# Order of the score matmuls in the middle blocks: all four heads' lower 64 keys first, then the upper 64

## The reference: what is computed

```
xq  = ada_ln(x_q,  t_vec, Wss_q,  bss_q)        # layer norm, then scale and bias from silu(cond)
xkv = ada_ln(x_kv, t_vec, Wss_kv, bss_kv)
q   = (xq @ Wq + bq)    -> (1, 4096, 16, 32)
k,v = (xkv @ Wkv + bkv) -> (1, 3202, 16, 32) each
scores = einsum('bqhd,bkhd->bhqk', q, k) / sqrt(32)
attn   = softmax(scores)
out    = x_q + (einsum('bhqk,bkhd->bqhd', attn, v) @ Wp + bp)
```

## Time and profile before

| what | value |
|---|---|
| median of 3 runs | 2154.9 us (2151.96 to 2155.5) |
| the profiled execution | 2154.18 us |
| its span, first to last instruction | 2152.5 us |
| TensorE busy | 2123.1 us (99%) |
| VectorE busy | 1925.8 us (89%) |
| ScalarE busy | 1801.6 us (84%) |
| score matmuls, line 1119 | 12800, busy 920.8 us |
| value matmuls, line 1131 | 6400, busy 853.3 us |
| exponentials, line 1377 | 1600, 1112 ns each |

### The profile page before, as it was taken

The page is one execution under the profiler, slowest core; times in us unless marked ns, Lnnn a source line. Parts: engine busy times, 40 slices in busy tenths (PEclk is TensorE's granted clock), DMA queues, the critical chain, the costliest instruction groups (busy, mean ns, idle before and its releaser), DMA issues.

```text
span 2152.5 us, 56243 instructions
## 1 busy us (share of the span) xinstructions
PE 2123.1 (99%) x25034; PEld 610.7 (28%) x25034; DVE 1925.8 (89%) x1193; ACT 1801.6 (84%) x1923; POOL 17.3 (1%) x28
## 2 busy tenths in 40 slices
PE   7999999999999999999999999999999999999998
PEld 3544322222222222222222222222222222222222
DVE  2335599999999999999999999999999999999998
ACT  1212599999999999999999999999999999999995
POOL 0001000000000000000000000000000000000000
PEclk9999999999999999999999999999999999999999
DMA  8346624223422324223422333233422332232321
GB/s 288 118 149 225 177 73 104 77 77 89 124 67 82 93 74 103 83 72 104 109 82 71 101 95 92 62 84 91 120 77 75 94 96 81 68 85 79 97 55 51
DMA packets 202212, 212.33 MB, mean 99 GB/s; under 512 B 18791, under 2 KB 136175, under 8 KB 201965
## 3 DMA queue, kind: packets, MB, share of 16 engines
q1 hardware_dynamic: 199420, 208.16, 34.6%
q10 hardware_dynamic: 2544, 0.53, 0.1%
HBM read 170.38 MB, written 38.26 MB: 97 GB/s over the span
## 4 chain that ended last, share of the span: by engine, by line
PE 97%; DVE 1%; DMA 1%; issue 0%; SPq 0%; ACT 0%; POOL 0%; ACTq 0%; DVEq 0%
PE bank L1119 40%; PE bank L1131 37%; PE bank L1189 5%; PE bank L1151 5%; PE bank L1035 4%; PE bank L1046 4%; PE bank L1162 1%; PE bank L1015 1%; PE bank L1247 1%; DVE stats L1473 0%; PE bank L1174 0%; DVE arena L1491 0%; DMA x_normal<-arena 0%; DMA arena<-in_ctx_dram 0%; PE bank L988 0%
## 5 line engine op out<-in xcount | busy, mean ns | idle before, releaser
L1377 ACT ACTIVATE arena<-bank,shift 128x1024 f32<-128x1024 f32 x1600 | 1691.7, 1112 | 140.7 <-PE bank L1119 133.8
L1694 DVE TENSOR_TENSOR arena<-arena 128x2048 f32<-128x2048 f32 x736 | 1641.4, 2283 | 67.4 <-ACT arena L1377 65.6
L1119 PE MATMUL bank<-qs,ks 32*64 32x512 f32 x12800 | 920.8, 613 | 4.6 <-ACT arena L1377 4.0
L1131 PE MATMUL bank<-arena,vg 128*32 128x512 f32 x6400 | 853.3, 605 | 1.2 <-ACT arena L1377 1.2
L1131 PEld LDWEIGHTS bank<-arena,vg 128*32 128x32 f32 x6400 | 126.0, 108 | 652.1 <-ACT arena L1377 650.5
L1119 PEld LDWEIGHTS bank<-qs,ks 32*64 32x64 f32 x12800 | 205.7, 130 | 371.0 <-ACT arena L1377 228.1
L1189 PE MATMUL bank<-wp,arena 128*32 128x168 f32 (+2 forms) x2464 | 153.6, 321 | 0.0
L1151 PE MATMUL bank<-xt,wq 128*32 128x256 f32 (+2 forms) x2016 | 143.0, 355 | 0.0
L1189 PEld LDWEIGHTS bank<-wp,arena 128*32 128x32 f32 x2464 | 80.1, 110 | 184.3 <-issue 165.3
L1334 ACT ACTIVATE arena<-bank,bk_c 128x512 f32<-128x512 f32 (+1 forms) x28 | 18.0, 642 | 130.4 <-PE bank L1035 124.1
L1151 PEld LDWEIGHTS bank<-xt,wq 128*32 128x32 f32 x2016 | 65.5, 110 | 150.8 <-issue 132.9
(11 more groups left out here) (89 smaller groups left out, 394.8 us busy)
## 6 DMA issues: line engine op xcount, KB each, us to landing
ks<-k_full SPq DMA_DIRECT2D x160, 320.0 KB, 3.1
vg<-v_full SPq DMA_DIRECT2D x160, 320.0 KB, 3.8
p_b<-p_tails SPq DMA_DIRECT2D x128, 128.0 KB, 4.2
arena<-in_x_dram SPq DMA_DIRECT2D x15, 1024.0 KB, 9.8
q_full<-qs SPq DMA_DIRECT2D x32, 256.0 KB, 2.0
out_dram<-arena SPq DMA_DIRECT2D x32, 256.0 KB, 2.2
x_normal<-arena SPq DMA_DIRECT2D x7, 1024.0 KB, 7.6
xin<-x_normal SPq DMA_DIRECT2D x28, 256.0 KB, 10.3
```

The source lines that it names most:

```text
L1119: mm = nc.tensor.matmul(bank[out, 2 * (i % RING) + h % 2, :], ks[rows_of(h), keys], qs[rows_of(h), g, :], start=True, stop=True)
L1131: mm = nc.tensor.matmul(bank[rows_of(h), o_bank(u), :], vg[:, t, rows_of(h)], pt[t % PR][:, h, :], start=(t == 0), stop=False, skip_group_ ...
L1377: nc.scalar.activation(pt[t % PR][:, 2 * pair:2 * pair + 2, :], bank[:, first:first + 2, :], ACT.Exp, scale=SCALE, bias=shift[:, g:g + 1]) ...
L1694: nc.vector.tensor_tensor(a[:, :, :], (pt[t - 1] if k <= 2 else a)[:, :, :], pt[t % PR][:, :, :], ALU.add).then_inc(p_added, 1)
```

## The change

In blocks 1 to 6 the 8 score matmuls of a step are written in another order. Before: wait for pair 0's banks, heads 0 and 1 of the lower side, heads 0 and 1 of the upper side, wait for pair 1's banks, heads 2 and 3 of the lower side, heads 2 and 3 of the upper side. Now: wait for pair 0's banks, heads 0 and 1 of the lower side, wait for pair 1's banks, heads 2 and 3 of the lower side, heads 0 and 1 of the upper side, heads 2 and 3 of the upper side. `s_ready` is still raised by each pair's last matmul. Blocks 0 and 7 keep the old order; the number of matmuls, their shapes and tiles, and the waits stay.

```diff
-                        for pair in range(2):
+
+                        def score(pair, side):
                             i = n + pair
-                            if i >= RING:
-                                pe.wait_ge(e_done, i - RING + 1)
-                            for side in range(2):
-                                out = slice(side * P // 2, (side + 1) * P // 2)
-                                keys = slice(t * P + side * P // 2, t * P + (side + 1) * P // 2)
-                                for h in (2 * pair, 2 * pair + 1):
-                                    mm = nc.tensor.matmul(bank[out, 2 * (i % RING) + h % 2, :], ks[rows_of(h), keys],
-                                                          qs[rows_of(h), g, :], start=True, stop=True)
-                            mm.then_inc(s_ready, 1)
+                            out = slice(side * P // 2, (side + 1) * P // 2)
+                            keys = slice(t * P + side * P // 2, t * P + (side + 1) * P // 2)
+                            for h in (2 * pair, 2 * pair + 1):
+                                mm = nc.tensor.matmul(bank[out, 2 * (i % RING) + h % 2, :], ks[rows_of(h), keys],
+                                                      qs[rows_of(h), g, :], start=True, stop=True)
+                            if side == 1:
+                                mm.then_inc(s_ready, 1)
+
+                        def banks_free(pair):
+                            if n + pair >= RING:
+                                pe.wait_ge(e_done, n + pair - RING + 1)
+
+                        if 1 <= u // NG < NB - 1:
+                            for pair in range(2):
+                                banks_free(pair)
+                                score(pair, 0)
+                            for pair in range(2):
+                                score(pair, 1)
+                        else:
+                            for pair in range(2):
+                                banks_free(pair)
+                                for side in range(2):
+                                    score(pair, side)
```

## The result

The changed kernel takes 2165.49 us (median of 6 runs, 2161.0 to 2166.99) against 2154.9 us (6 runs, 2151.96 to 2156.34): ratio 1.005, 95% interval 1.004 to 1.006, so 10.6 us slower. The profiled execution has a span of 2163.0 us, 10.5 more than before. The forecast was 2161.7 us, 6.8 more than before; the terms of its sum come to 7.2.

A forecast was written before the change was run, and what follows sets the result against it. TensorE was taken as the bound, short steps held up by a 2.32 us loop through ScalarE's exponential. 2154.18 + 6.4 + 0.8 = 2161.4 us, stated as 2161.7; own range 2157.5 to 2165, 8-in-10 range 2154 to 2168.

The forecast's parts named there:

- The loop of 2.32 us: Scores' start to pair 0's exponential 1.15 us, exponential 1.12, then 0.05 until the next step's pair 1 may start.
- the lost alternation: At unit changes in blocks 1 to 6, held-up and free steps would stop alternating; each behind a short one waits: 6.4 us.
- The 168-column steps lose their margin: In 192 steps with a 168-column side job, pair 1's banks would come free slightly late: 4 ns each, 0.8 us together.
- 2 x 0.007 = 0.014 us later: Pair 0's last score matmul, now sixth instead of fourth, would come this much later, making the loop 2.335 us.
- Unhindered steps unchanged: In some 530 steps without a hold-up the new order would change nothing; zero taken, a gain at most 14 us.
- Rival B: Four heads on four row groups first make the score passes shorter: 14.3 us gained, 2147 us in all; chance 0.07.
- Rival A: Heads 0 and 1 of the upper side pass the waiting head 2, so no change: 2155 us; chance 0.10.
- Rival C: In 66 held-up steps one head's two sides clash on the same rows: 11 us more, 2173 us; chance 0.07.
- VectorE and ScalarE have slack: Behind held-up steps neither engine's work would come due; they work 57.12 and 54.92 us of a 59.30 us unit.

The follow-up runs named there:

- third-place wait: Changed kernel with the old matmul order back in blocks 1 to 6, the wait for pair 1's banks still ahead of the third matmul: 2158.07 us, ratio 1.0024.
- the fifth and the seventh place: Changed kernel with pair 0's last score matmul fifth or seventh of eight in blocks 1 to 6, not sixth: 2160.01 and 2166.77 us.
- head-by-head order: Kernel before, all blocks, each head's lower and upper side written together, pair 0 whole ahead of the wait for pair 1's banks: 2153.45 us, ratio 1.0003.

## Why the prediction was right, and where its size was off

- *The loop of 2.32 us and the lost alternation*: shown. The changed kernel's steps behind short ones, the third-place wait and the new order in all blocks each show it. The term was 6.4 us; the steps themselves give 7.1, the new order for tiles 0 to 2 alone 6.4. What was missing is the first hold-up of each unit, which costs 0.31 us (2.35 - 2.04) instead of 0.28: the exponential ahead of it starts at 1.19 us, not 1.17. That the later hold-ups came out right is in part luck. The forecast added 0.015 us for the later place and took off 0.014 for the third matmul's own start. In the trace the place does not count behind the wait: pair 0's last matmul is the fourth to go after it, so the loop is the old one, 1.155 + 1.116 + 0.053 = 2.324 us.
- *"The 168-column steps lose their margin", 0.8 us, with ends of 0 and 1.9*: this is the term that failed. It measured 3.1 us, 16 ns a step and not 4, and the same cause took 0.6 us more from the steps of 176 columns and those behind them, which the forecast put at nothing. (The new order for tiles 3 to 24 gives 3.3 for both together and 0.6 for what it adds to the first hold-up.) The failed step is "2 x 0.007 = 0.014 us later": it took the pitch at which matmuls start for the pitch at which ScalarE can start on them. That pitch is 16.7 ns, 0.033 us for two places. Pair 1's banks then come free at 1.188 + 1.118 + 0.053 - 2.325 = 0.034 us into a 168-column step, while the third matmul is due at 0.014. So the step is held up by 0.02 and its length grows by 0.026 (2.35). It alternates once more, for another reason: a hold-up this small does not delay pair 0's exponential, which starts 1.19 us after the step in both kinds (1090.63 to 1091.82, 1092.96 to 1094.15), since 0.034 us and the 1.155 of a fourth place make 1.189 too. The second 168-column step of each unit loses 0.05 us (2.38), 1.2 of the 3.1 us: the exponential of pair 0 ahead of it starts 1.21 us after its step (1087.14 against 1085.93) and takes 1.13, right behind ScalarE's copy of the denominators (`l_sb`). The same copy in the kernel before and in the changed one:

```profile
1082.17 0.60 ACT L1393 ACTIVATE l_sb<-bank 128x512 f32<-128x512 f32 x1
1086.66 0.60 ACT L1408 ACTIVATE l_sb<-bank 128x512 f32<-128x512 f32 x1
1087.14 1.13 ACT L1392 ACTIVATE arena<-bank,shift 128x1024 f32<-128x1024 f32 x1
```

The forecast did not have that. Worse, the step that it read for all 192, at 1083.80, is this special one: the exponential ahead of it starts 1.17 us after its step (1082.64 against 1081.47), the others 1.156. The stated upper end had no row behind it either: a margin this thin should have been priced from the nearest hold-up.

- *Unhindered steps unchanged, zero taken from a range down to -14 us*: right, 2.04 us stands. Rival B is out.
- *Rival A (others pass the waiting one)*: out, 12 loads waited together. *Rival C (one head's two sides clash out of step)*: out. The clash that it prices would have made the held-up steps 0.17 us longer than the loop's 2.32, that is 2.49; they are 2.32 and 2.35.
- *VectorE and ScalarE have slack*: right; their busy time in the unit grew by 0.2 each and the unit by 0.53.

The total was 2161.7 forecast and 2165.5 measured, inside the range of 2154 to 2168 but outside the forecast's own 2157.5 to 2165. The sum has a slip besides: 2161.4 and the 0.7 us from the profiled execution to the median are 2162.1, not 2161.7. The mechanism of the larger term was right; the size of the change, 10.6 us, was not: of the 3.6 us by which the steps' 10.8 exceed the forecast's 7.2, 2.3 lie in the 168-column steps, 0.6 in those of 176 columns and 0.7 in the first hold-ups, and all three grow with the place of pair 0's last matmul, as the fifth and the seventh place show.

## What to carry to other kernels

Where a pair's consumer starts on its last matmul, put all of that pair ahead of any wait for something else: a wait in its midst hands every stall on to the consumer, and a stall that hit every second step then hits each. To find such a loop, lay the lengths of neighbouring steps side by side; steps with the same instructions and two lengths are its sign. And ask how far each steady wait is from becoming late: here a margin of 0.02 us on 192 steps was worth 3.1 us, and a little more on those of 176 columns.

## What the runs showed of the hardware

Matmuls on different tiles of the array start about 7 ns apart, but ScalarE can start on them 16.7 ns apart, for the fourth to the seventh of eight. The trace also holds the times at which TensorE raises `s_ready`, and they place this on TensorE's side. In unhindered steps pair 0's raise comes 1.132, 1.148, 1.165 and 1.182 us after the step's start, for the fourth to the seventh place, and ScalarE starts 0.023 us behind it each time. Pair 1's raise, on the eighth matmul, comes at 1.224 us in every order: 0.042 us behind the seventh, so 26 ns more than a place. Whether these go with a second raise or with the last place was not tested. Behind a wait the count begins anew: in the changed kernel's held-up step the loads go on at 1066.97 and the exponential starts at 1068.12, 1.15 us later, as for a fourth place. Why the two pitches differ was not settled. It is not the rows or columns: neighbours that share the array's rows cost the same as neighbours that share its columns.

The Trainium skill ("TensorE: Matmul & The Clock Gate", "The mechanism" of Part 3) lets a weight load overlap only matmuls of another row group. These runs do not bear that out: in the head-by-head order every second load has the row group of the matmul ahead of it, and the 16 loads of a step lie within the first 0.23 us, while its first matmuls run 0.64 us. That order ran at 1.0003 of the kernel before.

```profile
1102.32 0.23 PEld L1116 LDWEIGHTS bank<-qs,ks 32*64 32x64 f32 x16 [0.41 <-ACT arena L1390]
```
